# An own order of TensorE's work for the last attention unit of a fused attention and expert layer

## The chip, the cores and the metric

The kernel runs on one core of a Trainium2 chip. The metric is the device time of one execution in microseconds (us). One core has five engines that run their own instruction streams and wait for each other by semaphores: TensorE (PE), VectorE (DVE), ScalarE (ACT), GpSimd (POOL) and SyncE (SP), which here issues the DMAs.

## The reference

The layer is a pre-norm attention block with a residual, and a routed expert block with a residual. x is 4 x 1024 x 128 in float32, with 16 heads of 8.

```python
x = x + attn(layernorm(x))     # causal, 16 heads, softmax, output projection Wo, bo
# experts, top 1 of 8:
h, out = layernorm(x), 0
logits = h @ gate_w.T
sel, rw = argmax(logits), sigmoid(max(logits))
for e in range(8):
    xs = h * (rw * (sel == e))[:, None]
    out += (xs @ w_up[e].T) * silu(xs @ w_gate[e].T) @ w_down[e].T
x = x + out
```

## The kernel before

**Units.** The attention runs in 16 units, each of four heads of one batch; the last is unit 15. A unit has 12 slots: 4 blocks of 128 keys against the first 512 queries, and 8 against the second 512. Blocks on the diagonal have 512, 384, 256 and 128 query columns. These are slots 0 to 3 (first half) and 8 to 11 (second half); slots 4 to 7 have 512 columns. For each slot, in order:

- TensorE makes the scores, in *loads*: one head of 512 or 384 columns each (four loads a slot), or two heads together where the slot has 256 or 128 (two loads a slot). A unit has 40 loads, written here L0 to L39 (`load`, L1175, bf16). They take turns between the two halves of the array's rows, and between three banks of PSUM, so that load n waits until the exponential of load n-3 is done.
- ScalarE makes the exponential of each load (L768) in the order of loads, into one of four `prob` buffers.
- GpSimd masks the four heads of a diagonal slot once all its exponentials are done (L645, two instructions a slot).
- TensorE multiplies the slot with the values, written V0 to V11 (`values`, L1191, float32, 8 matmuls of 9 columns of weights). V0-V3 fill one PSUM bank, V4-V11 the same bank again. ScalarE copies it to `sum_sb` (`take_sums`, L759): that of V8-V11 of the unit before behind the exponentials of slot 0, and that of V0-V3 behind the exponentials of slot 5 (L19). V4 waits for the latter copy.

**The order.** The string `ORDER` sets the order of TensorE's work in every unit. S is the next load. V is the next values; its first three are the last three slots of the unit before (written V9', V10', V11' here), so that the last three slots of the last unit stand at its end. P is a piece of the next unit's search for the greatest scores, which VectorE reduces. a turns the second half of the maxima of this unit (T, L1151); VectorE copies it (L897) and SyncE sends it by two DMAs (L394) to the rows that L12 reads. In the last unit P has nothing to do and is left out.

**The start of the expert block in the last unit.** There are eight steps of 512 tokens behind the units. What the first two steps need stands among the loads of unit 15, put there by `lead_in` and the numbers of `FRONT`, which count loads:

- Q0-Q3 (`project3`, L1220, float32): the output projection of the first 512 tokens, a tile each. Q0 waits for VectorE's copy of T. VectorE then adds the residual and finds the moments and the ranks (`residual`, L960 to L974). GpSimd makes the scale (L663 to L666), ScalarE the tanh (L784), VectorE the weighed rows (L979, L982).
- Q4-Q7: the same for the next 512 tokens. They wait for the first moments. The first half's weighed rows are made before their residual.
- R (`spread_rank`, L1231): ranks are spread over partitions; ScalarE copies them (`copy_rank`, L789).
- X (`turn_xs`, L1037): weighed rows are transposed; ScalarE copies them (`copy_xs`, L793).

Behind the unit TensorE runs the steps, one behind another: gate matmuls (L1244), which wait for both copies, up (L1249), the projection of a later step (L1220), down (L1258). ScalarE's part of these, the silu (L808), waits for the last copy of the sums and for the load of its table.

Of the kernel before, what the change touches and what calls it, by code (L numbers as in the profile page):

```python
# [10 lines left out]
P = 128  # L11
# [6 lines left out]
TPH = HALF // P  # L18
# [3 lines left out]
UNITS = BATCH * HEADS // GH  # L22
# [18 lines left out]
Q = P // 2  # L41
# [3 lines left out]
SLOTS = [(c, j, max(0, Q * (j - TPH * c)), HALF - max(0, P * (j - TPH * c)))  # L45
         for c in range(2) for j in range(TPH * (c + 1))]
# [6 lines left out]
NL = len(LOADS)  # L53
# [16 lines left out]
NP = len(PIECES)  # L70
# [5 lines left out]
ORDER = "SPSPSSVVaVSSPPSSVSSSPVSSPSSPSSVSPSPSSVSPSVSPSSPVSSbSPSPSVSPSSVSSPSPSVSS"  # L76
LATE = 3
NB = 4


def unit_order(u):
    out = []
    seen = {"S": 0, "V": 0, "P": 0}
    for letter in ORDER:
        n = seen.get(letter, 0)
        seen[letter] = n + 1
        if letter == "S":
            out.append(("load", u, n))
        elif letter == "V":
            if n >= LATE:  # L90
                out.append(("values", u, n - LATE))
            elif u:
                out.append(("values", u - 1, len(SLOTS) - LATE + n))
        elif letter == "a":
            out.append(("turn", u, 1))
        elif u + 1 < UNITS:
            out.append(("piece", u + 1, n) if letter == "P" else ("turn", u + 1, 0))
    assert seen["S"] == NL and seen["V"] == len(SLOTS) and seen["P"] == NP
    if u == UNITS - 1:
        out += [("values", u, len(SLOTS) - LATE + n) for n in range(LATE)]  # L100
    return out

# [13 lines left out]
for n in range(NP):  # L116
# [3 lines left out]
    done, due = (AHEAD + -(-(len(EARLY) - AHEAD) * k // NP) for k in (n, n + 1))  # L120
    LEAD += EARLY[done:due]
ORDERS = [unit_order(u) for u in range(UNITS)]
USES = [e for e in LEAD + [e for o in ORDERS for e in o] if e[0] in ("piece", "turn")]
USE = {e: r for r, e in enumerate(USES)}
# [18 lines left out]
def layer_kernel(nc, x, wq_t, wk_t, wv_t, wo_t, bq, bk, bv, bo, bo_col, gate_t, wg_t, wu_t, wd_t, out):  # L143
# [7 lines left out]
    with ctx:  # L151
        def sb(name, shape, dt=FP32):
            return ctx.enter_context(nc.sbuf_tensor(name, shape, dt))
# [68 lines left out]
        rank = sb("rank", [P, 2, TPH], BF16)  # L222
        rank_b = sb("rank_b", [P, 2, HALF])
        weight = sb("weight", [P, 2, TPH])
        xs = sb("xs", [P, 2, TPH, DIM])
# [10 lines left out]
        def wide(banks):  # L236

            at = ps[:, banks[0]:banks[1] + 1, 0:2 * WIDE]
            return at.rearrange("p z (j c) -> p z j c", c=WIDE)
# [88 lines left out]
        def hold(eng, s, value):  # L328
            if value > 0:
                eng.wait_ge(s, value)  # L330
# [21 lines left out]
                              ).then_inc(rows_in[k], 16)  # L352


        FRONT = {"project_1": 7, "project_2": 16, "tanh": 22, "rank": 25, "turn": 29}
        block = ctx.enter_context(nc.Block())

        @block.sync
# [329 lines left out]
        def _(act):  # L688
# [93 lines left out]
            def tanh(n, h):  # L782
                act.wait_ge(scaled_set, n)
                a.activation(weight[:, h, :], scaled[:, h, :], ACT.Tanh).then_inc(tanh_set, 1)  # L784

            def copy_rank(n, h):
                act.wait_ge(rank_mm, n)
                hold(act, hidden_set, 4 * (n - 2))
                a.activation(rank_b[:, h, :], ps[:, BANK_RANK if n > 1 else FIRST_RANK, :], ACT.Copy).then_inc(rank_b_set, 1)  # L789

            def copy_xs(n, h):
                act.wait_ge(xs_turned, n)
                a.activation(xs_t[:, h, :], ps[:, BANK_TURN, :], ACT.Copy).then_inc(xs_t_set, 1)  # L793

            def lead_in(n):
                if n == FRONT["tanh"]:
                    tanh(1, 0)
                if n == FRONT["rank"] + 2:
                    copy_rank(1, 0)
                if n == FRONT["turn"] + 2:  # L800
                    copy_xs(1, 0)

            step(UNITS - 1, lead_in)

            def back(n4, pr):
# [225 lines left out]
        def _(pe):  # L1031
# [3 lines left out]
            def turn_tiles(src, bank):  # L1035
                for i in range(TPH):
                    last = nc.tensor.transpose(ps[:, bank, i * P:(i + 1) * P], src[:, i, :], ident[:])  # L1037
                return last
# [115 lines left out]
            def use(e):  # L1154
                kind, u, n = e
                r = USE[e]
                if kind == "turn":
                    pe.wait_ge(top_part_set, 2 * u + n + 1)
                elif n == 0:
                    pe.wait_ge(rows_in[u % 3], 192 * (u // 3 + 1))  # L1160
                hold(pe, use_free, r - 1)
                ins = piece(u, n, r) if kind == "piece" else turn(n, r)
                ins.then_inc(use_mm, 1)

            def load(u, n):
                i, rg, s, heads = LOADS[n]
                c, j, q0, cols = SLOTS[i]
                k = u % 3
                l = load_at(u, n)
                if n == SLOT_LOADS[i][0] and j == 0:  # L1170
                    pe.wait_ge(top_in[k][c], 32 * (u // 3 + 1))
                hold(pe, exp_done, l - 2)
                rows = slice(64 * rg, 64 * rg + ROWS_M)
                for m in range(heads):
                    last = mm(ps[:, l % 3, m * cols:(m + 1) * cols],  # L1175
                              k_rows[rows, k, j // TPH, s + m, j % TPH * P:(j % TPH + 1) * P],
                              q_rows[rows, k, c, s + m, q0:q0 + cols],
                              start=True, stop=True)
                last.then_inc(load_mm, 1)

            def values(u, i):
                c, j, q0, n = SLOTS[i]
                b, first_head = u // UPB, (u % UPB) * GH
                if j == 0:
                    hold(pe, sum_set, 2 * u + c)
                if i in DIAG:
                    pe.wait_ge(diag_done, diag_at(u, i))
                else:
                    pe.wait_ge(exp_done, slot_loaded(u, i))
                for g in range(GH):  # L1190
                    last = mm(ps[32 * g:32 * g + HD + 1, BANK_V, q0:q0 + n], v_all[:, b, j, first_head + g, :],  # L1191
                              prob[:, i % NB, g, 0:n], start=(j == 0), stop=(i == LAST[c]))
                last.then_inc(values_mm, 1)
# [22 lines left out]
            def project3(n, h, tiles=range(TPH)):  # L1216
                if tiles[0] == 0:
                    pe.wait_ge(attn_set, n)
                for i in tiles:
                    last = mm(wide(BANKS_PROJ)[:, i // 2, i % 2, :], attn[:, h, i * P:(i + 1) * P], w_o[:],  # L1220
                              start=True, stop=True)
                if tiles[-1] == TPH - 1:
                    last.then_inc(proj_mm, 1)

            def spread_rank(n, h):

                pe.wait_ge(rank_set, n)
                bank = BANK_RANK if n > 1 else FIRST_RANK
                hold(pe, silu_set, 4 * (n - 1) - 1)
                for i in range(TPH):  # L1230
                    last = mm(ps[:, bank, i * P:(i + 1) * P], rank[:, h, i:i + 1].to_broadcast((P, P)),  # L1231
                              ident_b[:], start=True, stop=True)
                last.then_inc(rank_mm, 1)

            def turn_xs(n, h):
                pe.wait_ge(xs_set, n)
                turn_tiles(xs[:, h], BANK_TURN).then_inc(xs_turned, 1)
# [23 lines left out]
                if prs[-1] == PAIRS - 1:  # L1261
                    last.then_inc(down_mm, 1)

            def lead_in(n):
                if n == FRONT["project_1"]:
                    pe.wait_ge(const_set, 4)
                    pe.wait_ge(use_free, len(USES))
                    pe.wait_ge(weights_in, 16 * 3)
                if n == FRONT["project_2"]:

                    pe.wait_ge(moments3, 1)
                if n == FRONT["rank"]:
                    spread_rank(1, 0)
                if n == FRONT["turn"]:
                    turn_xs(1, 0)
                for i in range(TPH):

                    if n == FRONT["project_1"] + i:
                        project3(1, 0, range(i, i + 1))
                    if n == FRONT["project_2"] + i:  # L1280
                        project3(2, 1, range(i, i + 1))

            for u in range(UNITS):
                for e in ORDERS[u]:
                    if e[0] == "load":
                        load(u, e[2])
                        if u == UNITS - 1:
                            lead_in(e[2])
                    elif e[0] == "values":
                        values(e[1], e[2])  # L1290
                    else:
                        use(e)
# [58 lines left out]
```

## Time and profile before

| what | value |
|---|---|
| median of 3 runs | 525.75 us (525.52 to 526.53) |
| the profiled execution | 523.49 us, span 521.8 us |
| PE busy in the span | 493.5 us (95%) |
| DVE, ACT, POOL busy | 441.8 (85%), 376.4 (72%), 225.7 us (43%) |
| mean granted TensorE clock | 0.992 |
| first gate matmul, behind the last unit | at 424.12 us |

The span runs from the first to the last instruction of the profiled execution. All times in the trace are counted from its start. Busy time of PE is by modelled ends: a matmul's row ends when its last column has drained, and the next may start before. So a cost is better read from one start to the next. The timeline merges instructions of one kind that follow each other; its rows tell the start, the time to the end of the last one, and how many there are. An L has one matmul for a head, a V has 8, a Q has 2.

### The profile page before, as it was taken

The numbers are of one execution on the slowest core, as the hardware profiler recorded it, in microseconds if no ns is written. First come the engines' busy times: TensorE is split into PE (matmuls) and PEld (weight loads), VectorE is DVE, ScalarE is ACT, GpSimd is POOL, SyncE is SP. The second block draws the span as 40 slices with busy tenths as digits, with TensorE's granted clock in tenths as the row PEclk, the third lists the DMA queues.
The fourth block names the chain that finished last, engine by engine and source line by source line (L and its number), as shares of the span: only waits on it lengthen the run. The fifth ranks groups of instructions, "written<-read, shape, count | busy, mean of one in ns | idle before, by whom it ended". The sixth has DMA issues, their size and how long they took to land.

```text
span 521.8 us, 12773 instructions
## 1 busy us (share of the span) xinstructions
PE 493.5 (95%) x4797; PEld 218.2 (42%) x4797; DVE 441.8 (85%) x695; ACT 376.4 (72%) x790; POOL 225.7 (43%) x526
## 2 busy tenths in 40 slices
PE   7699799999999999999999999999999899999997
PEld 6565324333332433324333332433333236777764
DVE  6958799999999999999998999999995428888864
ACT  7254698888989888898888989888797872222321
POOL 5397266353453635446363444634344142222210
PEclk9889999999999999999999999999999999999999
DMA  6252023422203232221423202112030212221001
GB/s 176 58 137 62 12 74 80 103 62 76 74 19 96 69 92 63 28 71 30 107 60 78 74 10 68 40 53 69 13 94 19 61 39 67 61 63 62 20 22 40
DMA packets 33550, 32.63 MB, mean 63 GB/s; under 512 B 10448, under 2 KB 26960, under 8 KB 33488
## 3 DMA queue, kind: packets, MB, share of 16 engines
q1 hardware_dynamic: 33376, 31.48, 22.8%
q8 instruction: 38, 0.62, 0.5%
q10 hardware_dynamic: 112, 0.33, 0.2%
q14 instruction: 24, 0.20, 0.1%
HBM read 20.26 MB, written 11.01 MB: 60 GB/s over the span
## 4 chain that ended last, share of the span: by engine, by line
PE 59%; DVE 30%; POOL 3%; ACT 3%; issue 3%; DMA 1%; ACTq 0%; DVEq 0%; POOLq 0%
PE ps L1191 18%; DVE top_p L890 11%; PE ps L1175 10%; PE ps L1136 8%; DVE top_p L885 7%; DVE top_p L887 6%; PE ps L1258 5%; PE ps L1244 5%; PE ps L1249 5%; POOL xn L564 2%; ACT sum_sb L759 2%; PE ps L1220 2%; DVE top L906 2%; PE ps L1144 2%; ACT prob L768 1%
## 5 line engine op out<-in xcount | busy, mean ns | idle before, releaser
L768 ACT ACTIVATE prob<-ps 128x512 f32<-128x512 f32 (+2 forms) x640 | 303.9, 564 | 35.1 <-PE ps L1175 33.6
L645 POOL TENSOR_SCALAR_AFFINE_SELECT prob<-prob 128x256 f32<-128x256 f32 x256 | 99.8, 417 | 181.4 <-ACT prob L768 178.6
L1175 PE MATMUL ps<-q_rows,k_rows 51*128 51x512 bf16 (+3 forms) x768 | 170.8, 328 | 3.3 <-ACT prob L768 1.6
L1191 PE MATMUL ps<-prob,v_all 128*9 128x512 f32 (+3 forms) x1536 | 156.9, 488 | 2.3 <-POOL prob L645 0.7
L885 DVE TENSOR_REDUCE top_p<-ps 128x2 f32<-128x1024 f32 x128 | 150.9, 1220 | 9.6 <-PE ps L1136 8.6
L1136 PE MATMUL ps<-k_rows,q_rows 48*128 48x128 bf16 (+3 forms) x1024 | 113.3, 265 | 7.4 <-DVE top_p L890 4.5
L1175 PEld LDWEIGHTS ps<-q_rows,k_rows 51*128 51x128 bf16 x768 | 53.0, 94 | 148.2 <-ACT prob L768 131.3
L890 DVE TENSOR_REDUCE top_p<-ps 128x8 f32<-128x1024 f32 x64 | 76.6, 1220 | 10.7 <-PE ps L1144 10.2
L887 DVE TENSOR_REDUCE top_p<-ps 128x4 f32<-128x1024 f32 x64 | 75.2, 1215 | 1.8 <-PE ps L1136 1.8
L1136 PEld LDWEIGHTS ps<-k_rows,q_rows 48*128 48x128 bf16 x1024 | 45.4, 94 | 27.2 <-DVE top_p L890 9.0
L1191 PEld LDWEIGHTS ps<-prob,v_all 128*9 128x9 f32 x1536 | 24.3, 88 | 52.2 <-issue 29.5
L808 ACT ACTIVATE prob<-ps 128x512 f32<-128x512 f32 x32 | 19.1, 597 | 32.7 <-PE ps L1244 20.1
L991 DVE SCALAR_TENSOR_TENSOR prob<-rank_b,rank_of,prob 128x512 f32<-128x512 f32 x32 | 23.3, 750 | 16.1 <-ACT prob L808 15.3
L1244 PE MATMUL ps<-xs_t,w_g 128*128 128x512 f32 x64 | 31.6, 596 | 0.0
L1249 PE MATMUL ps<-xs_t,w_u 128*128 128x512 f32 x64 | 31.4, 592 | 0.0
L1258 PE MATMUL ps<-w_d,prob 128*128 128x128 f32 x256 | 31.0, 275 | 0.0
L1258 PEld LDWEIGHTS ps<-w_d,prob 128*128 128x128 f32 x256 | 29.9, 192 | 1.0 <-issue 1.0
L1144 PE MATMUL ps<-shade,pick 64*128 64x256 bf16 (+1 forms) x160 | 29.4, 296 | 0.0
L759 ACT ACTIVATE sum_sb<-ps 128x512 f32<-128x512 f32 x32 | 19.0, 594 | 13.4 <-PE ps L1191 13.4
L663 POOL TENSOR_SCALAR spread<-moments 128x4 f32<-128x4 f32 x8 | 1.6, 195 | 55.4 <-DVE moments L969 55.3
L892 DVE TENSOR_REDUCE top_p<-ps 128x16 f32<-128x1024 f32 x16 | 19.5, 1221 | 6.8 <-PE ps L1144 6.4
L789 ACT ACTIVATE rank_b<-ps 128x512 f32<-128x512 f32 x8 | 4.8, 600 | 27.5 <-PE ps L1231 27.5
(110 smaller groups left out, 451.8 us busy)
## 6 DMA issues: line engine op xcount, KB each, us to landing
split_parts<-part SPq DMA_DIRECT2D x12, 384.0 KB, 4.4
q_rows<-split_parts SPq DMA_DIRECT2D x31, 96.0 KB
k_rows<-split_parts SPq DMA_DIRECT2D x31, 96.0 KB
value_sums<-sum_sb SPq DMA_DIRECT2D x128, 18.0 KB
x_sb<-x SPq DMA_DIRECT2D x8, 256.0 KB, 4.2
qk<-value_sums SPq DMA_DIRECT2D x8, 256.0 KB, 3.6
qk<-inverse_sums SPq DMA_DIRECT2D x8, 256.0 KB, 4.0
out<-y SPq DMA_DIRECT2D x8, 256.0 KB, 2.3
```

The source lines that it names most:

```text
L645: last = g.affine_select(out=quarter, in_=quarter, pattern=[[0, GH], [1, Q]], base=Q * (1 - z), channel_multiplier=-1, compare_op=ALU.is_g ...
L768: a.activation(prob[:, i % NB, g0:g0 + heads, 0:cols], ps[:, load_at(u, n) % 3, 0:heads * cols].rearrange("p (s t) -> p s t", s=heads), AC ...
L885: return v.tensor_reduce(top_p[:, c, place, s:s + 3:2, m], banks, AX.X, ALU.max)
L887: return v.tensor_reduce(top_p[:, c, place, :, m], banks.rearrange("p r (s t) -> p (r s) t", s=2), AX.X, ALU.max)
L890: return v.tensor_reduce(top_p[:, c, place, :, :].rearrange("p g m -> p (g m)"), banks.rearrange("p r (y t) -> p (r y) t", t=P), AX.X, ALU ...
L1136: last = mm(ps[:, first_bank + rg, cols], q_rows[rows, k, c, s, q0:q0 + P], k_rows[rows, k, 0 if width == HALF else c, s, k0:k0 + width], ...
L1144: last = mm(dst, pick[rows, PICK[tile]:PICK[tile] + P], shade[rows, None, :].to_broadcast((64, len(blocks), Q)), start=False, stop=True, s ...
L1175: last = mm(ps[:, l % 3, m * cols:(m + 1) * cols], k_rows[rows, k, j // TPH, s + m, j % TPH * P:(j % TPH + 1) * P], q_rows[rows, k, c, s + ...
L1191: last = mm(ps[32 * g:32 * g + HD + 1, BANK_V, q0:q0 + n], v_all[:, b, j, first_head + g, :], prob[:, i % NB, g, 0:n], start=(j == 0), sto ...
L1244: mm(ps[:, BANK_GATE[pr % 2], :], w_g[:, pr * P:(pr + 1) * P], xs_t[:, h, :], start=True, stop=True).then_inc(gate_mm, 1)
L1249: mm(ps[:, BANK_UP[pr % 2], :], w_u[:, pr * P:(pr + 1) * P], xs_t[:, h, :], start=True, stop=True).then_inc(up_mm, 1)
L1258: last = mm(ps[:, BANK_DOWN, i * P:(i + 1) * P], hidden[:, pr, i * P:(i + 1) * P], w_d[:, pr, :], start=(pr == 0 and i == 0), stop=(pr == ...
```

## The change

`unit_order` gets a second string, `LAST_ORDER`, for the last unit alone. It has letters for the projection tiles (Q), the ranks (R) and the turned rows (X), so `lead_in` of TensorE goes, and a function `project_tile` keeps its waits. The numbers of `FRONT` now serve ScalarE alone: its tanh stands behind the exponential of L25 (before: L22), and its copies of ranks and turned rows both behind that of L39 (before: L27 and L31). The instructions are the same ones, in number and size.

```diff
+LAST_ORDER = "SVSSVSVSaSSQQSQQSSSVSSSSVSSVSSRSSVQQSSVSSSVSSVSSSVSSXSSQSSQSSSV"
 def unit_order(u):
     out = []
-    seen = {"S": 0, "V": 0, "P": 0}
-    for letter in ORDER:
+    last = u == UNITS - 1
+    seen = {"S": 0, "V": 0, "P": 0, "Q": 0}
+    for letter in LAST_ORDER if last else ORDER:
...
+        elif letter == "Q":
+            out.append(("project", u, n))
+        elif letter in "RX":
+            out.append(({"R": "rank", "X": "xs"}[letter], u, 0))
...
-        FRONT = {"project_1": 7, "project_2": 16, "tanh": 22, "rank": 25, "turn": 29}
+        FRONT = {"tanh": 25, "rank": 39, "turn": 39}
...
-                if n == FRONT["rank"] + 2:
+                if n == FRONT["rank"]:
                     copy_rank(1, 0)
-                if n == FRONT["turn"] + 2:
+                if n == FRONT["turn"]:
                     copy_xs(1, 0)
...
-            def lead_in(n):
-                if n == FRONT["project_1"]:
+            def project_tile(n):
+                if n == 0:
                     pe.wait_ge(const_set, 4)
                     pe.wait_ge(use_free, len(USES))
                     pe.wait_ge(weights_in, 16 * 3)
-                if n == FRONT["project_2"]:
+                if n == TPH:
                     pe.wait_ge(moments3, 1)
...
+                project3(1 + n // TPH, n // TPH, range(n % TPH, n % TPH + 1))
```

The order of TensorE in the last unit, whole. Before:

L0 L1 L2 L3 V9' V10' T V11' L4 L5 L6 L7 Q0 V0 L8 Q1 L9 Q2 L10 Q3 V1 L11 L12 L13 L14 L15 L16 Q4 V2 L17 Q5 L18 Q6 L19 Q7 L20 V3 L21 L22 V4 L23 L24 L25 R V5 L26 L27 L28 L29 X L30 V6 L31 L32 L33 V7 L34 L35 L36 L37 V8 L38 L39 V9 V10 V11

After:

L0 V9' L1 L2 V10' L3 V11' L4 T L5 L6 Q0 Q1 L7 Q2 Q3 L8 L9 L10 V0 L11 L12 L13 L14 V1 L15 L16 V2 L17 L18 R L19 L20 V3 Q4 Q5 L21 L22 V4 L23 L24 L25 V5 L26 L27 V6 L28 L29 L30 V7 L31 L32 X L33 L34 Q6 L35 L36 Q7 L37 L38 L39 V8 V9 V10 V11

Below, `q_rows,k_rows` are loads, `prob,v_all` values, `w_o,rest` projection tiles, `top_part` T, `xs` X. Line numbers after the change are 10 higher. First, TensorE where the last unit begins (behind the last two loads of unit 14, which have 128 columns), before:

```order
L1175 MATMUL ps<-q_rows,k_rows 128x128 x4
L1175 MATMUL ps<-q_rows,k_rows 128x512 x4
L1191 MATMUL ps<-prob,v_all 9x384 x4
L1191 MATMUL ps<-prob,v_all 9x256 x4
L1151 MATMUL ps<-ident_b,top_part 48x128
L1191 MATMUL ps<-prob,v_all 9x128 x4
L1175 MATMUL ps<-q_rows,k_rows 128x384 x4
L1220 MATMUL ps<-w_o,rest 128x136
L1191 MATMUL ps<-prob,v_all 9x512 x4
```

And TensorE at the same place after:

```order
L1185 MATMUL ps<-q_rows,k_rows 128x128 x4
L1185 MATMUL ps<-q_rows,k_rows 128x512
L1201 MATMUL ps<-prob,v_all 9x384 x4
L1185 MATMUL ps<-q_rows,k_rows 128x512 x2
L1201 MATMUL ps<-prob,v_all 9x256 x4
L1185 MATMUL ps<-q_rows,k_rows 128x512
L1201 MATMUL ps<-prob,v_all 9x128 x4
L1185 MATMUL ps<-q_rows,k_rows 128x384
L1161 MATMUL ps<-ident_b,top_part 48x128
L1185 MATMUL ps<-q_rows,k_rows 128x384 x2
L1230 MATMUL ps<-w_o,rest 128x136 x2
```

The three values of the unit before went in between the first loads, and the first two projection tiles together in front of L7.

Second, TensorE at the end of the unit, from V7 to the first gate matmul, before:

```order
L1191 MATMUL ps<-prob,v_all 9x512 x4
L1175 MATMUL ps<-q_rows,k_rows 128x384 x2
L1175 MATMUL ps<-q_rows,k_rows 128x256 x4
L1191 MATMUL ps<-prob,v_all 9x512 x4
L1175 MATMUL ps<-q_rows,k_rows 128x128 x4
L1191 MATMUL ps<-prob,v_all 9x384 x4
L1191 MATMUL ps<-prob,v_all 9x256 x4
L1191 MATMUL ps<-prob,v_all 9x128 x4
L1244 MATMUL ps<-xs_t,w_g 128x512 x2
```

And TensorE there after, from X to V11:

```order
L1047 MATMUL ps<-ident,xs 128x128 x4
L1185 MATMUL ps<-q_rows,k_rows 128x384 x2
L1230 MATMUL ps<-w_o,rest 128x136
L1185 MATMUL ps<-q_rows,k_rows 128x384
L1185 MATMUL ps<-q_rows,k_rows 128x256 x2
L1230 MATMUL ps<-w_o,rest 128x136
L1185 MATMUL ps<-q_rows,k_rows 128x256 x2
L1185 MATMUL ps<-q_rows,k_rows 128x128 x4
L1201 MATMUL ps<-prob,v_all 9x512 x4
L1201 MATMUL ps<-prob,v_all 9x384 x4
L1201 MATMUL ps<-prob,v_all 9x256 x4
L1201 MATMUL ps<-prob,v_all 9x128 x4
```

X, Q6 and Q7 now stand among the loads of slots 9 to 11, and V8 (9x512) behind the last load.

Third, ScalarE at the end of the last unit, from the exponentials of slot 4 on, before:

```order
L759 ACTIVATE sum_sb<-ps 128x512
L768 ACTIVATE prob<-ps 128x512 x3
L784 ACTIVATE weight<-scaled 128x4
L768 ACTIVATE prob<-ps 128x512 x5
L789 ACTIVATE rank_b<-ps 128x512
L768 ACTIVATE prob<-ps 128x512 x4
L793 ACTIVATE xs_t<-ps 128x512
L768 ACTIVATE prob<-ps 128x384 x4
L768 ACTIVATE prob<-ps 128x2x256 x2
L768 ACTIVATE prob<-ps 128x2x128 x2
L759 ACTIVATE sum_sb<-ps 128x512
```

And ScalarE there after:

```order
L769 ACTIVATE sum_sb<-ps 128x512
L778 ACTIVATE prob<-ps 128x512 x6
L794 ACTIVATE weight<-scaled 128x4
L778 ACTIVATE prob<-ps 128x512 x6
L778 ACTIVATE prob<-ps 128x384 x4
L778 ACTIVATE prob<-ps 128x2x256 x2
L778 ACTIVATE prob<-ps 128x2x128 x2
L799 ACTIVATE rank_b<-ps 128x512
L803 ACTIVATE xs_t<-ps 128x512
L769 ACTIVATE sum_sb<-ps 128x512
```

The two copies left the exponentials and stand behind the last of them. The rows of VectorE, GpSimd and SyncE are the same before and after.

## Rows read from the trace of the kernel before

**Rows 1.** Windows: busy us (x count) of PE, PEld, DVE, ACT, POOL; PEclk; DMA.

```profile
395.60:424.10 28.50, 25.53 (x197) 8.05 (x197) 9.93 (x46) 21.88 (x47) 10.24 (x29) 1.00 0.19 49
424.10:436.30 12.20, 12.20 (x68) 8.14 (x65) 8.83 (x27) 5.34 (x9) 3.19 (x5) 1.00 0.05 11
```

**Rows 2.** Waits, 395.6 to 424.1: who <- whom: us in total, times, longest.

```profile
PEld ps L1175 <- ACT prob L768: 13.1, 22, 1.1
...
ACT prob L768 <- PE ps L1175: 4.0, 9, 1.0
```

**Rows 3.** Timeline of PE, start of the unit: start, us, what [idle <-releaser].

```profile
396.28 1.15 PE L1175 MATMUL ps<-q_rows,k_rows 51*128 51x512 bf16 x3 [0.23 <-ACT prob L768]
397.36 1.26 PE L1191 MATMUL ps<-prob,v_all 128*9 128x384 f32 x16
398.55 0.24 PE L1151 MATMUL ps<-ident_b,top_part 128*48 128x128 bf16 x1
398.72 0.41 PE L1191 MATMUL ps<-prob,v_all 128*9 128x128 f32 x8
...
400.23 0.33 PE L1175 MATMUL ps<-q_rows,k_rows 51*128 51x384 bf16 x1 [0.67 <-ACT prob L768]
```

**Rows 4.** Timeline of PE: L10, L17 to V4, and the unit's end.

```profile
403.40 0.28 PE L1175 MATMUL ps<-q_rows,k_rows 51*128 51x128 bf16 x2
...
407.84 0.39 PE L1175 MATMUL ps<-q_rows,k_rows 51*128 51x512 bf16 x1
408.15 0.50 PE L1220 MATMUL ps<-w_o,rest 128*128 128x136 f32 x2
408.59 0.39 PE L1175 MATMUL ps<-q_rows,k_rows 51*128 51x512 bf16 x1
...
410.74 0.39 PE L1175 MATMUL ps<-q_rows,k_rows 51*128 51x512 bf16 x2
411.52 1.04 PE L1191 MATMUL ps<-prob,v_all 128*9 128x512 f32 x8 [0.40 <-ACT sum_sb L759]
...
421.90 0.29 PE L1175 MATMUL ps<-q_rows,k_rows 51*128 51x128 bf16 x4
...
424.12 1.98 PE L1244 MATMUL ps<-xs_t,w_g 128*128 128x512 f32 x4
```

**Rows 5.** Timeline of PE behind the unit: four projection tiles in a row.

```profile
431.21 1.09 PE L1220 MATMUL ps<-w_o,rest 128*128 128x136 f32 x8
432.14 1.95 PE L1258 MATMUL ps<-w_d,prob 128*128 128x128 f32 x16
```

**Rows 6.** Timeline of ACT, 389 to 423: exponentials and one copy.

```profile
389.20 2.55 ACT L768 ACTIVATE prob<-ps 128x512 f32<-128x512 f32 x5 [0.43 <-PE ps L1175]
...
399.19 0.60 ACT L759 ACTIVATE sum_sb<-ps 128x512 f32<-128x512 f32 x1 [0.74 <-PE ps L1191]
399.69 1.64 ACT L768 ACTIVATE prob<-ps 128x384 f32<-128x384 f32 x4
...
422.22 0.66 ACT L768 ACTIVATE prob<-ps 128x256 f32<-128x256 f32 x2 [0.31 <-PE ps L1175]
```

**Rows 7.** Timeline of POOL, DVE, SP; then issues of DMAs, KB, us to landing.

```profile
396.56 0.78 POOL L645 TENSOR_SCALAR_AFFINE_SELECT prob<-prob 128x256 f32<-128x256 f32 x2 [0.19 <-ACT prob L768]
...
422.95 0.78 POOL L645 TENSOR_SCALAR_AFFINE_SELECT prob<-prob 128x256 f32<-128x256 f32 x2 [0.18 <-ACT prob L768]
...
404.24 0.19 DVE L960 TENSOR_TENSOR logit<-ps,gate_q 128x32 f32<-128x32 f32 x1 [4.42 <-PE ps L1220]
...
406.06 0.38 DVE L969 BATCH_NORM_AGGREGATE moments<-stats 128x2 f32<-128x6 f32 x4
...
400.62 1.51 SPq L400 DMA_DIRECT2D value_sums<-sum_sb  x4
...
inverse_sums<-inv SPq DMA_DIRECT2D x2, 64.0 KB, 1.6
...
qk<-value_sums SPq DMA_DIRECT2D x2, 256.0 KB, 3.9
```

More of the change, by code:

```diff
@@ L95, in unit_order @@
             out.append(("turn", u, 1))
+        elif letter == "Q":
+            out.append(("project", u, n))
+        elif letter in "RX":
+            out.append(({"R": "rank", "X": "xs"}[letter], u, 0))
         elif u + 1 < UNITS:
             out.append(("piece", u + 1, n) if letter == "P" else ("turn", u + 1, 0))
-    assert seen["S"] == NL and seen["V"] == len(SLOTS) and seen["P"] == NP
-    if u == UNITS - 1:
+    assert seen["S"] == NL and seen["V"] == len(SLOTS)
+    assert seen["Q"] == 2 * TPH if last else seen["P"] == NP
+    if last:
         out += [("values", u, len(SLOTS) - LATE + n) for n in range(LATE)]
@@ L1268, in lead_in @@
                     pe.wait_ge(weights_in, 16 * 3)
-                if n == FRONT["project_2"]:
+                if n == TPH:
                     pe.wait_ge(moments3, 1)
[L1272 to L1281, printed above, removed]
+                project3(1 + n // TPH, n // TPH, range(n % TPH, n % TPH + 1))
             for u in range(UNITS):
@@ L1286, in _ @@
                         load(u, e[2])
-                        if u == UNITS - 1:
-                            lead_in(e[2])
+                    elif e[0] == "project":
+                        project_tile(e[2])
+                    elif e[0] == "rank":
+                        spread_rank(1, 0)
+                    elif e[0] == "xs":
+                        turn_xs(1, 0)
                     elif e[0] == "values":
```

## The prediction

> **What bounds the kernel now.** I read the busy shares by stretch first, then who waited for whom in the last unit, then TensorE's timeline row by row, and last the other engines beside it. From 424.1 on TensorE is busy for all of 12.20 us out of 12.20, so the end of the program hangs on when the first gate matmul starts, at 424.12; what follows is one unbroken row of matmuls. In the last unit, 395.6 to 424.1, it is busy for 25.53 of 28.50 us by the modelled ends [rows 1], and those ends include the drain of each matmul, so the real slack is larger. In this stretch it waited mostly for ScalarE's exponentials, 22 times, and ScalarE in its turn 9 times for loads [rows 2]: neither engine is full, each waits for the other. VectorE, which set the pace of the units before, has no more pieces to reduce here. So the question is how much of 28.45 us (395.67, the start of L0, to 424.12) a new order saves; all else moves along with it.
>
> **What each step costs TensorE**, from start to start:
> - L alone, then another form: 0.32 us (407.84 to 408.15, 512 columns); 2x128 columns 0.21. Two L in a row stream side by side: two of 128x2 columns are one row of 0.29 us where one alone is 0.28, and L21 and L22 of 512 columns are one row of 0.39, as is one alone [rows 4]. A pair so costs 0.22 us, plus 0.10 when another form follows.
> - V: 0.98 / 0.76 / 0.55 / 0.34 us for 512 / 384 / 256 / 128 columns, 0.11 less when another V follows (V9', V10' and T: 397.36 to 398.55) [rows 3, 4].
> - Q alone 0.43 us (408.15 to 408.59) [rows 4]. Four in a row take 0.93 [rows 5], 0.23 for each one that follows another; a pair is 0.66.
> - T 0.17, R 0.34, X 0.59.
>
> Each change of form (L, V, Q, T, R, X) so costs about 0.10 us: an L of 512 columns streams in 0.21 of its 0.32.
>
> **Work and waits before.** 40 L in 17 runs 6.93, 15 V in 12 runs 10.50, 8 single Q 3.45, T, R and X 1.10: together 21.98 us. The rest, 6.5 us, is waiting: in L0-L3 1.1 (each waits for an exponential, while V9' stands behind them), L4-L7 1.0 (L7 waits, since ScalarE had sat 0.74 us for V11' before it could copy the sums and do the exponential of L4) [rows 3, 6], L11-L16 1.3, L21-L25 0.7 (V4 waits for the copy of the sums, 0.40 of it) [rows 4], L26-L29 0.8, L34-L37 1.0 (exponentials again), and V9-V11 0.6 for GpSimd's last mask, which ends at 423.73 [rows 7]; these parts are read off the starts of the same timeline, and their sum is the rest of the 28.45.
>
> **The change, part by part.**
> 1. V9', V10', V11' move between L0, L1/L2 and L3. They are ready (the last of the three masks ends at 397.34 [rows 7]), and fill what L0-L3 waited. V11' ends at 398.3 in place of 399.1, so the copy of the sums starts at 398.6 in place of 399.19 [rows 6] and L7's wait goes.
> 2. Q0-Q3 and Q4, Q5 go in pairs: 8 singles cost 3.45, the new 3 pairs and 2 singles 2.85: -0.6 us.
> 3. V2, V6 and V7 come earlier, and V8 later: in the old order V8 stood before L38, and V9 to V11 then ran out of work before the mask of the last slot; now V8 (0.87) and V9 cover L39's exponential and its mask (0.78 [rows 7]).
> 4. Q6, Q7 and X stand among L32-L37, where TensorE waited 1.0 us.
> 5. ScalarE's copies of the ranks and turned rows (0.48 us of its cadence each) move from among the exponentials to behind the last one. There they end 1.42 us after its start; the mask of slot 11 and V11 need 0.38 + 0.08 + 0.78 + 0.06 + 0.34 = 1.64 [rows 6, 7]. So they are covered, by 0.2 us at least.
> 6. Q7 ends at 415.8 in place of 410.1. VectorE's residual starts 0.2 us behind and has its moments after 2.2 more (404.24 to 406.44 in the first half [rows 7]), at 418.2; GpSimd wants them only behind its last mask, 418.5. Covered, by 0.3 us, and tanh behind it has 1.2 more.
> 7. T comes one place later: its copy by VectorE ends 0.55 us after it, and L5 and L6 cover that but for 0.1 before Q0. The two sends to the rows of L12 are issued up to 400.62, as before.
>
> L costs 6.93 in the new order too (19 runs, two more changes, but more of them in pairs). Work: 21.38.
>
> **The walk.** I laid the new order end to end by these durations. L n starts 0.06 us after exponential n-3 ends (three banks); an exponential starts 0.42 us after its L (0.37 for 384 columns, 0.32 for 2x128) or when ScalarE is free, which takes 0.48 (512), 0.37 (384) or 0.28 (2x128) each and lasts 0.6, 0.5 or 0.38 [rows 6]; a masked slot is ready 0.9 us after its last exponential. TensorE starts:
>
> V9' 396.00, V10' 397.09, V11' 397.97, T 398.58, Q0 399.20, V0 401.25, L12 402.39, V1 403.31, V2 404.40, V3 406.45, Q4 406.79, V4 407.78, V5 409.35, V6 410.66, V7 412.22, X 413.53, Q7 415.37, L39 416.43, V8 416.66, V11 418.61, gate 418.83.
>
> Waits that are left: 0.17 at L5/L6, 0.53 in L11-L14 (four L with no V between), 0.5 in L17-L20, 0.2 in L33/L34, 0.4 in L37-L39, 0.1 elsewhere: 1.9 us. The same walk along the old order gives the gate at 423.96 where the trace has 424.12: 0.16 too early, which I add: 418.99.
>
> **The sum:** waits 6.5 to 1.9, -4.6 (-4.7 with the rounding of the walk); work -0.6; the walk's error +0.16: -5.1 us. The profiled execution has a span of 521.8 and took 523.5, the median is 525.75; I take the saving off each alike: span 516.7, time **520.6 us**. The bound above: with no wait at all TensorE would save 7.1.
>
> The page "TensorEngine Tiling (Array Packing)" of the Trainium skill, Key Properties, says that a change of tiling mode drains TensorE. By that rule alone the split of the L into 19 runs is a loss, and the order that keeps them together the better one; the trace prices a change at 0.10, so two more cost 0.2 against waits of 4.6, and the three paired Q give back more.
>
> **The rivals.**
> - *L's don't pair here* (8 in 100). If a pair behind an exponential only just done streamed one after the other, the same walk ends at 420.2, 1.4 later: saving 3.7, 522.1. Against it: L21/L22 and L38/L39 pair in the trace [rows 4]. For it: in the new order many second L's become ready only as the first one starts.
> - *L12 waits for its rows* (7 in 100). The sends are issued until 400.62 [rows 7]; small transfers land 1.6 us later [rows 7], 402.2, and L12 is due at 402.39. At 3.9 us, as loads of 256 KB take [rows 7], it would be 404.5 and L12 2.1 late: saving 3.0, 522.7. The page "DMA: Bandwidth & Descriptors" (Trainium skill), Anatomy of one DMA, gives about 2.0 us fixed cost for a transfer; by that L12 would be 0.2 late and the time 520.8; no run here shows it for this transfer.
> - *The new waits are worse than walked* (7 in 100): ScalarE has 18.6 us of work (28 x 0.48, 8 x 0.37, 4 x 0.28, two copies of 0.49, tanh) in 20.9, from its first exponential to the end of its last, and small delays no longer fall into slack. Half of the saved waits back: saving 2.8, 522.9.
> - *No effect* (3 in 100): the tail keeps its time because it waits for loads of attention rows. Against it: these are issued behind the copy of the sums of slot 3, which also comes 4 us earlier. 525.7.
> - *Slower* (2 in 100): the denser row of matmuls brings TensorE's granted clock down from the level of 2.4 to 1.2 GHz in the unit. Each us of work at the lower level costs one more; from 5.1 us of it on, the change loses, and the unit's 21.4 us of work at it would give 542. Against it: 1.00 was granted all through the unit and through the 12.20 us after it that are wholly busy [rows 1].
>
> **Numbers.** The forecast as such has 73 in 100, 519.8 to 521.5 by itself. The range reaches over the first two rivals and the measurement's own 0.2% (1 us, what can be told from no change here): 519.5 to 522.7. Faster by over 0.2%: 0.95 (the forecast and the first three rivals); within: 0.03; slower: 0.02.
>
> **What would show it.** In the profile after: the gate's first matmul 5.1 us earlier, near 419.0; the rest of the span unchanged at 97.7 us; the copy of the sums of the unit before at 398.6 with hardly any idle time before it; L7 unheld; V4 not held by the second copy of the sums; Q0/Q1, Q2/Q3 and Q4/Q5 in rows of x4; the last mask at 417.7. Wrong would be: a wait of L12 for a transfer, an idle stretch of TensorE between V11 and the gate, or tanh of the second half late and the second gate group with it.

## The result and the profile after

| comparison | before, median | changed, median | ratio (95% interval) |
|---|---|---|---|
| the one the prediction is held against | 525.91 us (4 runs) | 519.76 us (4 runs, 519.57 to 520.94) | 0.9877 (0.9852 to 0.9901) |
| `after_again` | 526.13 us (17 runs) | 519.89 us (6 runs, 518.37 to 520.47) | 0.9879 (0.9856 to 0.9901) |
| `after_third` | 525.64 us (17 runs) | 520.79 us (5 runs, 520.62 to 521.23) | 0.9907 (0.9882 to 0.9932) |

The change is faster. The first ratio, put on the 525.75 us of the prediction, gives 519.3 us: a saving of 6.5 us, where 5.1 was forecast and the range ended at 6.25 (519.5).

The trace says where the saving is. I cut the span of each profile at three marks: the first exponential of unit 1, the first exponential of unit 15, and the first gate matmul. Windows of the kernel before (stretch; its length, busy us and count of PE, PEld, DVE, ACT, POOL; PEclk, DMA share, GB/s):

```profile
0.00:80.72 80.72, 67.48 (x609) 39.83 (x611) 64.61 (x136) 48.57 (x103) 48.04 (x85) 0.96 0.35 91
80.72:396.38 315.66, 306.90 (x3513) 107.46 (x3510) 295.86 (x324) 277.35 (x589) 151.29 (x389) 1.00 0.24 62
396.38:424.12 27.74, 25.00 (x192) 7.83 (x191) 9.19 (x45) 21.34 (x46) 9.48 (x27) 1.00 0.19 50
424.12:521.76 97.64, 94.13 (x492) 63.05 (x488) 72.14 (x192) 29.15 (x55) 16.93 (x26) 0.99 0.16 46
```

The same four stretches of the changed kernel:

```profile
0.00:82.29 82.29, 70.33 (x609) 41.43 (x611) 64.72 (x136) 48.35 (x103) 47.98 (x85) 0.94 0.34 89
82.29:397.99 315.70, 307.13 (x3520) 107.49 (x3517) 295.91 (x324) 277.35 (x589) 151.14 (x389) 1.00 0.24 62
397.99:420.41 22.42, 22.16 (x192) 7.92 (x185) 9.50 (x45) 20.92 (x46) 9.46 (x27) 1.00 0.22 62
420.41:518.07 97.66, 94.13 (x492) 63.04 (x488) 72.17 (x193) 29.14 (x55) 16.89 (x26) 0.99 0.16 46
```

The second and the fourth stretch agree to 0.04 us. The last unit takes 22.42 us in place of 27.74: 5.32 us less, with TensorE busy for 22.16 of them. The first stretch took 1.57 us longer in this profile, at a lower mean clock, so the two spans differ by 3.7 us only. The 5.32 us of the unit are the effect of the change; the first stretch, in which nothing was changed, is where executions differ (below).

Inside the unit, TensorE's timeline of the changed kernel (start, us to the end of the last one, what, count). The first exponential of the unit comes 1.61 us later than in the profile before (397.99 and 396.38), so all times here are to be read 1.61 us earlier beside the prediction's:

```profile
397.58 0.83 PE L1201 MATMUL ps<-prob,v_all 128*9 128x384 f32 x8
398.35 0.39 PE L1185 MATMUL ps<-q_rows,k_rows 51*128 51x512 bf16 x2
398.67 0.62 PE L1201 MATMUL ps<-prob,v_all 128*9 128x256 f32 x8
399.22 0.39 PE L1185 MATMUL ps<-q_rows,k_rows 51*128 51x512 bf16 x1
399.54 0.41 PE L1201 MATMUL ps<-prob,v_all 128*9 128x128 f32 x8
399.88 0.33 PE L1185 MATMUL ps<-q_rows,k_rows 51*128 51x384 bf16 x1
400.14 0.24 PE L1161 MATMUL ps<-ident_b,top_part 128*48 128x128 bf16 x1
400.31 0.43 PE L1185 MATMUL ps<-q_rows,k_rows 51*128 51x384 bf16 x2
400.80 0.70 PE L1230 MATMUL ps<-w_o,rest 128*128 128x136 f32 x4
401.43 0.33 PE L1185 MATMUL ps<-q_rows,k_rows 51*128 51x384 bf16 x1
...
408.31 0.73 PE L1230 MATMUL ps<-w_o,rest 128*128 128x136 f32 x4
408.98 0.39 PE L1185 MATMUL ps<-q_rows,k_rows 51*128 51x512 bf16 x2
409.30 1.05 PE L1201 MATMUL ps<-prob,v_all 128*9 128x512 f32 x8
...
417.93 0.28 PE L1185 MATMUL ps<-q_rows,k_rows 51*128 51x128 bf16 x2 [0.20 <-ACT prob L778]
418.14 2.34 PE L1201 MATMUL ps<-prob,v_all 128*9 128x512 f32 x32
420.41 1.13 PE L1254 MATMUL ps<-xs_t,w_g 128*128 128x512 f32 x2
```

V9', V10' and V11' stand where TensorE had waited for exponentials [rows 3]. L7 (401.43) starts with no wait, where it had 0.67 us. The projection tiles go as x4, two tiles in one row. V4 (409.30) is no longer held by the copy of the sums, which had cost it 0.40 [rows 4]. V8 to V11 are one row of x32, with no gap for the last mask, and the gate follows.

Beside it ScalarE and GpSimd, in the same kernel:

```profile
400.22 0.62 ACT L769 ACTIVATE sum_sb<-ps 128x512 f32<-128x512 f32 x1
...
418.79 0.62 ACT L799 ACTIVATE rank_b<-ps 128x512 f32<-128x512 f32 x1
419.27 0.63 ACT L803 ACTIVATE xs_t<-ps 128x512 f32<-128x512 f32 x1
...
418.43 1.52 POOL L655 TENSOR_SCALAR_AFFINE_SELECT prob<-prob 128x256 f32<-128x256 f32 x4 [0.20 <-ACT prob L778]
```

The copy of the sums of unit 14 starts without the 0.74 us of idle time it had [rows 6]. The two moved copies end at 419.90, half a microsecond ahead of the gate. The last two slots are masked in one row that ends at 419.95, and V11 needs it at 420.08. The waits of the stretch shrank as well:

```profile
PEld ps L1185 <- ACT prob L778: 7.5, 14, 0.9
...
ACT prob L778 <- PE ps L1185: 1.3, 5, 0.4
```

Before, they were 13.1 us in 22 waits and 4.0 in 9 [rows 2]. The upper row counts the idle time of TensorE's weight loads (PEld), which is more than the matmuls lost: 13.1 us beside the 6.5 that TensorE waited by its starts.

### The profile page after: what moved, and what is told of

Its sections match the earlier page's. It is cut to its first block, busy times and chain, and to the rows that moved or that the text cites. A ratio compares the mean times of both kernels' runs of the same rounds, so it can differ in the third digit from the quotient of the medians.

```text
span 518.1 us, 12773 instructions
## 1 busy us (share of the span) xinstructions
PE 493.8 (95%) x4797; PEld 219.9 (42%) x4797; DVE 442.3 (85%) x695; ACT 375.8 (73%) x790; POOL 225.5 (44%) x526
## 4 chain that ended last, share of the span: by engine, by line
PE 62%; DVE 28%; ACT 4%; POOL 3%; issue 2%; ACTq 0%; POOLq 0%; DVEq 0%
PE ps L1201 19%; DVE top_p L900 10%; PE ps L1185 10%; PE ps L1146 8%; DVE top_p L895 7%; DVE top_p L897 6%; PE ps L1268 6%; PE ps L1254 5%; PE ps L1259 5%; POOL xn L574 2%; ACT sum_sb L769 2%; DVE top L916 2%; PE ps L1154 1%; PE ps L1230 1%; ACT prob L778 1%
```

## The experiments

Two questions were open: do the parts cost what the walk says, and where is the 0.8 to 1.2 us that the medians and the ratio show beyond the unit's 5.3? Each kernel's last unit is read as above, from its first exponential to the first gate matmul. "Walk" is the one of the prediction, laid along the order of that kernel; its own 22.45 us for the changed kernel met 22.42. Where an expectation names the old order's walk, it is 27.57 where the trace has 27.74. Every diff below is against the changed kernel, also where the run is the old order with one part changed; `FRONT = {"tanh": 22, "rank": 27, "turn": 31}` puts ScalarE's copies where the kernel before had them. Most of these kernels were run once, so they are judged by the unit in their profile and not by their time.

### One more of each: the time outside the unit

> The kernel before once more, unchanged, to see how its executions differ among themselves. Two theories for the part of the saving (6.2 us by the medians) that the last unit does not hold (5.3 us from the first exponential of the unit to the first gate matmul, 27.74 to 22.42). Theory A, the clock: executions differ in stretches of lower granted TensorE clock ahead of the last unit (one more of 3.4 us at 62.5 us in the profile after), and the medians compare different numbers of them. It expects spans from 521.8 to 525, the longer ones at a lower mean clock or with a later start of the units, and 27.7 us in the unit in each profile. Theory B, the program: the changed kernel runs its early part faster, each time. It expects the span of this one never under 523.5 and its units ahead of the last one later than those of the changed kernel.

> The changed kernel once more. Theory A expects a ratio to before nearer to the unit's own saving, 5.3 of 525.8 us, 0.990, with spans that differ from run to run by about 1 us; theory B expects 0.988 again and the early part faster in the profile. Both expect 22.4 us from the unit's first exponential to the first gate matmul.

> The kernel before, one more profile. In both profiles of it the last unit took 27.73 us from its first exponential to the gate, units 1 to 14 took 315.6 and the tail 97.6; only the time up to unit 1 differed (80.72 and 84.04 us), with 0 and 10.2 us of lower clock around 60 us. If the whole difference between executions is ahead of unit 1, this one has 27.7 again, and a span of 521.8 plus what it loses there. If instead the order of before now and then loses the clock within the last unit, as the kernel with the start alone did once (6.8 us at 409.6, 29.48 us in the unit in place of 27.3), this one may show 28 to 31 us there.

> The changed kernel a third time, for its spread: of 10 executions so far none had a mean clock under 0.987, where 7 of 29 of the kernel before did. If the old order now and then loses the clock in the last unit and the new one does not, this one again has no execution under 0.987, and the ratio stays at 0.988; if the losses lie ahead of unit 1 for both, it shows some, and the ratio goes to 0.990. The unit has 22.4 us in either case.

The windows of `before_again` and `after_again`, the first and the third stretch of each (`before_third` had 82.49 and 27.74 us, `after_third` 83.29 and 22.41):

```profile
0.00:84.04 84.04, 72.38 (x609) 41.89 (x611) 64.78 (x136) 48.39 (x102) 47.92 (x85) 0.90 0.34 87
...
399.69:427.42 27.73, 24.99 (x193) 7.82 (x192) 9.17 (x45) 21.33 (x46) 9.45 (x27) 1.00 0.18 50
```

```profile
0.00:82.97 82.97, 69.52 (x609) 39.86 (x611) 64.88 (x136) 48.24 (x102) 48.03 (x85) 0.94 0.34 88
...
398.61:421.02 22.41, 22.15 (x192) 7.91 (x184) 9.49 (x45) 20.92 (x46) 9.47 (x27) 1.00 0.21 62
```

The unit takes 27.73 to 27.74 us in all three profiles of the old order and 22.41 to 22.42 in all three of the new one. The first stretch goes from 80.7 to 84.0 with the old order, at a mean clock of 0.96 down to 0.90, and from 82.3 to 83.3 with the new one. With the other kernels of this study it was 81.3 to 84.6, so it does not follow the change. Theory A stands in its main part: what differs between executions lies ahead of unit 1. Theory B falls: the early part of the changed kernel is not the faster one.

Theory A also names the clock, and the mean over the first stretch does not settle that: the shortest one (80.72 us, `before`) has 0.96, the longest (84.61 us, `v8_early`) 0.94. The part from the first exponential of unit 0 to that of unit 1 does; here it is for `before`, `singles`, `v8_early` and `before_again`:

```profile
58.23:80.72 22.49, 20.39 (x244) 7.25 (x238) 20.65 (x22) 19.51 (x42) 12.57 (x22) 1.00 0.28 73
58.85:81.34 22.49, 20.39 (x242) 7.17 (x236) 20.65 (x22) 19.51 (x41) 12.54 (x22) 1.00 0.29 73
60.78:84.61 23.83, 21.91 (x244) 7.50 (x238) 20.74 (x22) 19.52 (x42) 12.54 (x22) 0.93 0.27 70
58.79:84.04 25.25, 24.58 (x244) 8.66 (x241) 20.82 (x22) 19.51 (x41) 12.55 (x22) 0.81 0.26 65
```

At a clock of 1.00 unit 0 took 22.49 us in both profiles that had it, and with a lower mean clock 23.6 to 25.3 in the other twelve. What stands ahead of unit 0 took 58.2 to 59.1 us in 13 of the 14 profiles. Only in `v8_early` was it 60.8; there TensorE waited 1.9 us for a DMA of `k_rows` at 32.5, in place of 0.3 in `before`.

The two kernels timed again and again show how much that matters. The unchanged copy, against the kernel before in the same comparison, came out at 0.9993 (0.9971 to 1.0014), but single executions of it ran from 523.41 to 530.16 us. The changed kernel's ratio was 0.9879 in one comparison and 0.9907 in the next, on either side of the 0.9899 that the unit's 5.32 us of 525.9 would give. All 58 executions of the old order in this study have a median of 525.86 us, all 15 of the new one 520.39: 5.5 us less, though they come from different comparisons. The further guess, that the old order sometimes loses the clock in the last unit, was not seen in any of its three profiles; and of the changed kernel's five executions in `after_third` two had a mean clock of 0.986 and 0.983, where none of the ten before had been under 0.987. That, and the ratio of 0.9907, is what the expectation gave for losses ahead of unit 1 in both kernels. (It counts 7 of 29 executions of the kernel before under 0.987; on record are 6 of 29.) What remains of the first two ratios beyond 0.990 is within their intervals. Only one execution of each has a profile (519.78 and 520.39 us), and their first stretches (82.29 and 82.97 us) lie among those of the old order; so it is argued and not shown that the spread of the executions made this rest.

### The start alone

```diff
-LAST_ORDER = "SVSSVSVSaSSQQSQQSSSVSSSSVSSVSSRSSVQQSSVSSSVSSVSSSVSSXSSQSSQSSSV"
+LAST_ORDER = "SVSSVSVSaSSSQVSQSQSQVSSSSSSQVSQSQSQSVSSVSSSRVSSSSXSVSSSVSSSSVSS"
-        FRONT = {"tanh": 25, "rank": 39, "turn": 39}
+        FRONT = {"tanh": 22, "rank": 27, "turn": 31}
```

> One part alone: the order of before, but with V9', V10', V11' between L0 and L4 and T behind L4. The walk of the prediction (gate at a time after the first exponential; 27.57 for the order of before, where the trace has 27.74) gives 27.09: 0.5 us less than before. A rival, that the values of the unit before are what held ScalarE and all else followed from it, expects most of the 5.3 us from this part alone.

> The kernel with the start alone once more, timed. Its first profile had 6.8 us of lower clock at 409.6, inside the last unit. The walk gives 27.1 us for the unit, with its error on the old order 27.25. If the loss of the clock in the unit belongs to this order, its profile shows it again and many executions have a mean clock of 0.984 or less and take over 526; if it was one execution's, the profile has 27.25 us in the unit and the executions lie 0.5 us under those of before (ratio 0.999).

The first run's unit took 29.48 us, but at a mean clock of 0.88. The second gave a clean one. The two windows, `start_only` first:

```profile
398.13:427.61 29.48, 27.30 (x193) 8.24 (x185) 9.19 (x45) 21.43 (x46) 9.46 (x27) 0.88 0.16 47
```

```profile
399.32:426.49 27.17, 24.67 (x192) 7.77 (x184) 9.19 (x45) 21.33 (x46) 9.48 (x27) 1.00 0.19 51
```

So 27.17 where 27.25 was expected: the start alone saves 0.57 us of the 5.32. The rival, that all followed from it, falls. Timed, it is 0.9999 (0.9980 to 1.0018) of before: 0.57 us can't be told that way. The 2.3 us that the first run lost stand at 409.6, in one profiled execution of two. They do not belong to this order: two of its twelve timed executions had a mean clock of 0.984 or less, and three of the 17 of the kernel before in the same comparison.

### The pairs alone

```diff
-LAST_ORDER = "SVSSVSVSaSSQQSQQSSSVSSSSVSSVSSRSSVQQSSVSSSVSSVSSSVSSXSSQSSQSSSV"
+LAST_ORDER = "SSSSVVaVSSSSQQVSSQQSVSSSSSSQQVSSQQSSVSSVSSSRVSSSSXSVSSSVSSSSVSS"
-        FRONT = {"tanh": 25, "rank": 39, "turn": 39}
+        FRONT = {"tanh": 22, "rank": 27, "turn": 31}
```

> One part alone: the order of before, but with Q0/Q1, Q2/Q3, Q4/Q5, Q6/Q7 in pairs. By the price of a Q in the prediction alone, 0.2 us for each pair, it would save 0.8 us. The walk gives 26.03, 1.5 us less than its 27.57 for before, since the loads between them pair too. The rival that only the waits count expects under 0.3.

```profile
398.46:424.58 26.12, 23.68 (x192) 7.46 (x192) 9.25 (x45) 20.80 (x46) 9.48 (x27) 1.00 0.20 53
```

26.12 us: 1.62 less than before, twice the 0.8 that the tiles alone give, as the walk had it (1.5). PE is busy 1.3 us less by the modelled ends. Two tiles together leave two loads together, and those stream side by side: L17 and L18 take 0.32 us from their start to that of Q6 (409.44 to 409.76), as one alone does.

### The pairs taken out of the new order

```diff
-LAST_ORDER = "SVSSVSVSaSSQQSQQSSSVSSSSVSSVSSRSSVQQSSVSSSVSSVSSSVSSXSSQSSQSSSV"
+LAST_ORDER = "SVSSVSVSaSSQSQSQSQSVSSSSVSSVSSRSSVQSQSVSSSVSSVSSSVSSXSSQSSQSSSV"
```

> The new order with the projection tiles taken apart again: Q0 L7 Q1 L8 Q2 L9 Q3 L10, and Q4 L21 Q5 L22; all else as in the changed kernel. The prediction's price (0.2 us for each of three pairs) expects 0.6 us more than the 22.42 of the changed kernel. The walk gives 23.83, 1.4 more, since the loads between them lose their partners too. The rival that only the place of V and of the waits matters expects under 0.2 more.

```profile
397.04:420.80 23.76, 23.23 (x193) 8.09 (x185) 9.50 (x45) 21.07 (x46) 9.48 (x27) 1.00 0.22 58
```

23.76 us, 1.34 more than the changed kernel (walk: 1.38). The timeline of `singles`, from L7 to L10, shows what the changed kernel with its pairs does not pay:

```profile
400.32 0.33 PE L1185 MATMUL ps<-q_rows,k_rows 51*128 51x384 bf16 x1
400.59 0.50 PE L1230 MATMUL ps<-w_o,rest 128*128 128x136 f32 x2
401.02 0.39 PE L1185 MATMUL ps<-q_rows,k_rows 51*128 51x256 bf16 x2
...
402.52 0.28 PE L1185 MATMUL ps<-q_rows,k_rows 51*128 51x128 bf16 x2
```

Each load between two tiles takes its full time from start to start (0.27 us for L7 with 384 columns, 0.32 for L8 and L9, 0.21 for the short L10), each tile 0.43 (Q0 0.47). Q0 to V0, with four tiles and L7 to L10, takes 2.88 us (399.85 to 402.73); in the changed kernel the same work took 1.99 (400.80 to 402.79).

### V8 early, and the copies at their old places

```diff
-LAST_ORDER = "SVSSVSVSaSSQQSQQSSSVSSSSVSSVSSRSSVQQSSVSSSVSSVSSSVSSXSSQSSQSSSV"
+LAST_ORDER = "SVSSVSVSaSSQQSQQSSSVSSSSVSSVSSRSSVQQSSVSSSVSSVSSSVSSXSSQSSQSVSS"
```

> The new order with V8 back in front of L38. The walk gives 22.84, 0.4 us more than the changed kernel's 22.45 in the walk, since V9 to V11 then run out of work before the mask of slot 11 is done; then TensorE waits some 0.5 us at V11. If masks do not limit the end, no difference.

```profile
400.31:423.17 22.86, 22.40 (x192) 7.66 (x184) 9.44 (x45) 21.03 (x46) 9.43 (x27) 1.00 0.22 61
```

22.86 us, 0.44 more, and the wait is where it was expected (0.40 us); GpSimd's last mask (422.00 to 422.78) now holds V11 in the timeline of `v8_early`:

```profile
421.18 1.26 PE L1201 MATMUL ps<-prob,v_all 128*9 128x384 f32 x16
422.84 0.41 PE L1201 MATMUL ps<-prob,v_all 128*9 128x128 f32 x8 [0.40 <-POOL prob L655]
```

The second run of this section keeps TensorE's new order and puts back ScalarE's copies and its tanh:

```diff
-        FRONT = {"tanh": 25, "rank": 39, "turn": 39}
+        FRONT = {"tanh": 22, "rank": 27, "turn": 31}
```

> The new order of TensorE with ScalarE's tanh and copies at their old places (behind L22, L27 and L31). The walk gives 22.97 us, 0.5 more than its 22.45 for the changed kernel: the copy of the turned rows has to wait for X, which now stands behind L32, and holds the exponentials behind it. If the places of the copies cost nothing, 22.4.

```profile
399.52:422.58 23.06, 22.58 (x193) 7.88 (x185) 9.42 (x45) 20.87 (x46) 9.39 (x26) 1.00 0.21 60
```

23.06 us, 0.64 more than the changed kernel, where the walk had 0.52. The copy of the turned rows does wait for X and holds the exponentials behind it, and with them the loads. In its timeline, X on TensorE, L35 and L36 with the wait before them, and the copy on ScalarE:

```profile
416.72 0.66 PE L1047 MATMUL ps<-ident,xs 128*128 128x128 f32 x4
418.45 0.77 PE L1185 MATMUL ps<-q_rows,k_rows 51*128 51x384 bf16 x3 [0.25 <-ACT prob L778]
...
417.42 0.60 ACT L803 ACTIVATE xs_t<-ps 128x512 f32<-128x512 f32 x1
```

The places of the copies matter, and behind the last exponential they do not hold the gate. The tanh was put back in the same run; its own share was not measured.

### Loads of one half in a row

```diff
-LOADS.sort(key=lambda l: (l[0], l[2], l[1]))
+LOADS.sort(key=lambda l: (l[0], l[1], l[2]))
```

> The changed kernel with the four loads of a slot in the order of the array's row halves 0 0 1 1 in place of 0 1 0 1, in all units, so that the first and the second load of such a slot can't stream side by side. The rule that loads pair by halves gives 22.63 in the walk, 0.2 us more; if they never paired in this unit, no difference.

```profile
83.40:400.54 317.14, 310.99 (x3520) 107.00 (x3517) 295.86 (x324) 278.87 (x589) 151.24 (x389) 1.00 0.23 61
400.54:423.12 22.58, 22.32 (x192) 7.93 (x184) 9.61 (x46) 20.87 (x46) 9.47 (x27) 1.00 0.22 62
```

22.58 us, 0.17 more (walk: 0.18), and 1.4 us more over units 1 to 14 ahead (317.14 for 315.70). The row of L26 and L27, first in the changed kernel, then here:

```profile
411.90 0.39 PE L1185 MATMUL ps<-q_rows,k_rows 51*128 51x512 bf16 x2
```

```profile
414.44 0.60 PE L1185 MATMUL ps<-q_rows,k_rows 51*128 51x512 bf16 x2
```

Two loads of different halves end 0.39 us after the first one starts, two of the same half 0.60; V6 starts 0.32 us behind the first of them in the one kernel, 0.54 in the other. The page "TensorE: Matmul & The Clock Gate" of the Trainium skill, Part 3, The mechanism, says that tiles at different row positions overlap; the trace agrees, with 0.39 us for these and 0.60 for two at the same position.

### A searched order

```diff
-LAST_ORDER = "SVSSVSVSaSSQQSQQSSSVSSSSVSSVSSRSSVQQSSVSSSVSSVSSSVSSXSSQSSQSSSV"
+LAST_ORDER = "SVSSVSVaSSSQQQSSQSSVSSSVSSVSSRSSVQQSSSVSSXSSVSSSVSSVSSSQSSSQSSV"
-        FRONT = {"tanh": 25, "rank": 39, "turn": 39}
+        FRONT = {"tanh": 19, "rank": 39, "turn": 39}
```

> Another order for the last unit, found by trying moves of letters against the walk: T, L5, L6, Q0, Q1, Q2, L7, L8, Q3 and V, R, X and Q6, Q7 at other places, tanh behind L19. The walk gives 22.16 us in the unit where the changed kernel has 22.45 in the walk and 22.41 in the trace: 0.3 us less. By the time alone it can't be told from the changed kernel; if orders are at their limit it is the same within 0.1.

```profile
398.50:420.66 22.16, 22.02 (x192) 7.82 (x184) 9.17 (x44) 20.73 (x46) 9.29 (x26) 1.00 0.23 63
```

(Its T stands in front of L4; L4 to L6 follow it.) 22.16 us, as the walk had it, 0.25 less than the changed kernel. By time it is 520.02 us and 0.9898 (0.9862 to 0.9934) of before: not to be told from the changed kernel. It beats it by its unit alone. There is little waiting left, as TensorE is busy for 22.02 of 22.16 us by the modelled ends; whether another order needs less than this for the work itself, no run tells.

Not every part of the change has a run of its own. Taken alone or taken out, the start is worth 0.57 us, the pairs 1.34, V8's place 0.44, the places of the copies and the tanh 0.64. The earlier V2, V6 and V7 (part 3 of the prediction's list) and Q6, Q7 and X among L32 to L37 (part 4) were tested only as part of the whole order, which the walk met.

## Why the prediction was right, and where it was wrong

- **What bounds** was right: the tail took 97.66 us in place of 97.64, and each microsecond saved in the unit came out whole.
- **The waits.** By the single starts of the trace 6.6 us of waits went to 1.9, where the prediction had 6.5 to 1.9, and at the same places: 0.21 at L5/L6 (0.17), 0.52 in L11-L14 (0.53), 0.5 in L17-L20 (0.5), 0.3 in L37-L39 (0.4).
- **The work.** The eight tiles took 2.82 us (2.85), V 10.47 (10.50). But the item "8 singles cost 3.45, the new ones 2.85" is only half of what pairing is worth. In `singles` it is 1.34 us and in `pairs_only` 1.62: the loads that the tiles had parted find partners. The prediction had this in its walk ("more of them in pairs") and not in its list of parts. The sum did not suffer from it: its total for the loads, 6.93 us, counts the new pairs, and what the trace's unit leaves for them is about 6.9.
- **The sum.** 5.13 us by the walk, 5.32 in the trace. The added 0.16 for the walk's error was the wrong correction: the error of the walk lay in the old order (27.57 for 27.74), not in the new one (22.45 for 22.42), so it should have been left out or taken the other way. With the trace for the old order and the walk for the new one, the forecast would have been a saving of 5.29. This term is 0.2 us off; by itself it does not bring the result out of the range.
- **The covers held**, by what was said: the moved copies, the residual of the second half (its moments end at 419.74, the mask at 419.95), V11's mask (0.13 us ahead of V11). L12 did not wait for its rows: it started 0.25 us behind L11, 0.09 after the exponential that its bank needs.
- **The step that failed is the lower edge of the range**, and with it the step from the unit to the time ("I take the saving off each alike"). The mechanism and the sum were right to 0.2 us: 5.1 us forecast for the unit, 5.32 measured. But the time was taken as a median less the unit's saving, and the first ratio gives 519.3 us, 1.3 below the forecast of 520.6 and 0.2 below the edge of 519.5. Even the measured 5.32 taken off 525.75 gives 520.4. The forecast by itself already reached down to 519.8, so the microsecond for the measurement was not added to this but laid over it: 0.3 us were left, where the interval of this one comparison is 1.3 us to each side. In place of a fixed median the runs show executions that differ ahead of unit 1: the first stretch alone went from 80.7 to 84.6 us in 13 profiles of kernels that agree in it (`same_half`, which has its loads in another order there too, had 83.4). The two later comparisons gave 0.9879 and 0.9907, which is 519.4 and 520.9 us on the same base, one outside the range again and one inside. Why the first two ratios came out below the unit's 0.9899 stays open; it lies inside both of their intervals.
- **The rivals.** That L's don't pair: they do, also behind an exponential (L26 and L27, 0.32 us from start to start); `same_half` shows what it costs in the unit where the first two and the last two of a slot's four can't, 0.17 us, where the rival's price for none of them pairing was 1.4. L12's rows: no wait. Counted as the prediction counts, from the end of the last issue, the rows were there within 1.84 us (402.17 to 404.01). The 2.0 us that it takes from the page "DMA: Bandwidth & Descriptors" of the Trainium skill stand there, under Anatomy of one DMA, for transfers that GpSimd issues; these are issued by SyncE, and the 0.2 us of delay reckoned from it did not come. Worse waits: no. No effect: no. The clock did fall to 0.50 once for 6.8 us in the last unit, in `start_only`, and cost 2.3 us there; so it can happen, but in the changed kernel none of three profiles shows it.

## What to carry to other kernels

Where two engines wait for each other by turns, read each step's cost from start to start and lay the new order by hand, with each wait; here that met the trace within 0.2 us for nine kernels, one of them found by it, while a list of single savings missed half of what pairing was worth. Group small matmuls of one form, both for their own sake and for the ones they would part. And judge a change of one stage by that stage in the trace; the ratio of whole times had an interval of 1.3 us to each side, while the unit repeated to 0.01 us. For the same reason, a range for the time needs the spread of the measurement on both sides, on top of the error of the sum.

## What the runs showed of the hardware

- The last unit of the same program took the same time to 0.01 us in three profiles, while the first 80 us differed by up to 3.9 us among kernels that agree there. Part of this goes with the granted clock of TensorE: unit 0 took 22.49 us twice at 1.00 (2.4 GHz), and 25.25 us in `before_again`, where from 60 to 67.5 us 0.50 was granted, the 1.2 GHz level.
- The clock can fall in a stretch in which TensorE has work for most of the time: in `start_only` it was granted 0.50 from 409.6 to 416.4 with PE busy 6.63 of 6.80 us, and another profile of the same kernel kept 1.00 there. I have no explanation.

```profile
409.60:416.40 6.80, 6.63 (x29) 1.82 (x29) 0.56 (x3) 3.79 (x8) 0.00 (x0) 0.50 0.06 11
```

- At that level V4 took 1.83 us from start to start in `start_only` (414.27 to 416.10) in place of 0.98, and a projection tile alone 0.76 (410.36 to 411.12) in place of 0.43.
